# Scale stores, row broadcasts and the first context load in another order on SyncE, with three buffers placed anew

## The chip, the core and the metric

The kernel runs on one core of a Trainium2 chip. The time is that of one execution on the device, in microseconds (us). The core has five engines with queues of their own, which meet only through semaphores: TensorE (PE in the profile; its weight loads are shown as PEld), VectorE (DVE), ScalarE (ACT), GpSimd (POOL) and SyncE (SP). SP does no arithmetic here; it issues nearly every DMA transfer, each at its place in a written order, and a wait in its order holds up all that stands behind. The transfers are then carried out by 16 DMA engines, whose queue is shared by all that SP issues.

## What is computed

x and the context are 16 batches of 64 tokens with 512 features (1024 tokens: 8 tiles of 128). Four residual steps follow one another:

```python
x = x + tanh(g_xattn[0]) * L0_xattn(layernorm(x), ctx, ctx, mask, wq, wk, wv, wo)   # 32 heads, 8 kv heads, rope
x = x + tanh(g_ffn[0])   * L0_ffn(layernorm(x), Wg, Wu, Wd)       # weights to 4 bits, activations to 8
x = x + tanh(g_xattn[1]) * L1_xattn(layernorm(x), ctx, Wq, bq, Wk, bk, Wv, bv)      # attention over channels
x = x + tanh(g_ffn[1])   * L1_ffn(layernorm(x), W_base, b_base, lora_A, lora_B, router_W, ...)
```

In L0_ffn each row of a weight has its own scale: `scale = max(|w|) / 7`, the row is rounded to integers, and the product is multiplied by the scale. There are 1376 rows in Wg, 1376 in Wu and 512 in Wd.

## The kernel before

The program has two blocks, and a barrier of all engines lies between them. The first, attention_block, computes the whole L0 attention, and in its gaps prepares the weights of the FFN and of the second layer. The second, tail_block, does the other three steps, tile by tile, in an order written out by hand for each engine.

**The slots of the first block.** Its main loop runs over 8 kv heads with two head pairs each (NPAIR is 16) and two halves of the tiles: 32 units, U = 0 to 31. In unit U, PE computes the output product of unit U - 1 (output, four tiles, each ended by L492 and counted in s_wo), transposes the probabilities of U (L608), takes the scores of U + 1 (L472), multiplies probabilities and v (L621), and then computes two or three projections for later units (L78 to L80). ScalarE copies the transposed probabilities out of PSUM (L827), the high part of the result (L832), and so on; VectorE adds the output product to x (accumulate, L939) and takes the low parts; GpSimd normalises and rotates.

**SP's order.** SP runs through slots V = 0 to 63, two to a unit. In each it may load the next piece of an FFN weight (load_piece, L326, into xn), store a finished quantised and transposed piece to a scratch tensor in DRAM (store_piece, L335 to L341), and load attention weights (next_weights, L278 to L290). Waits on semaphores in front of these tie it to the pace of the units. A few things have their place by number of slot: at V = 32 (2 * NPAIR), when all pieces of Wg and Wu are through, their scales go to DRAM: w_scale holds them in SBUF by partition, 10 columns of 128 and one of 96 for each weight, and the store writes every scale as an element of 4 bytes (L382, L385). At V = 53 come the small loads of the second layer (load_block1, L1284), and at V = 56 (4 * NPAIR - 8) the 512 scales of Wd (L391), in the same manner. After the loop SP issues the base weight of the last step (L1303, 1 MB; it counts to the same semaphore as the loads of load_block1), the three quantised weights (L398 to L400: w_T twice, wd_T), waits until PE has done the last projection (s_proj), loads tile 0 of the context for the second layer (load_context, L1429: four transfers of 128 KB, two for each parity into b_ctx), waits for the scale stores (s_p_row), and reads the scales back as rows that are broadcast to all partitions (L406: w_row twice, wd_row). At last it duplicates the first q and k (duplicate_tile, L1439) when VectorE has them.

**Who waits for these.** In unit 30, VectorE starts the selection of the experts (selection_of_experts, L1027) and PE the transposes of the small weights; both wait for all loads of load_block1 and the base weight. At the end of unit 30, ScalarE rounds both parities of the context to their high parts (first_split_hi, L801); GpSimd takes the low parts behind them (L1241), and then the inverse deviations (L1245) for which it needs VectorE. PE uses the result in the last output product (first_qk). The rows and quantised weights are used in the second block only.

**The end of the first block.** VectorE's last steps are first_lo_qk for both parities (L1063), the last three accumulates, and between the last two of them low_b_lo (L1069), which waits for ScalarE's low_b_hi (L797). low_b is read in the tail by lora. The first instruction of VectorE in the second block is front_tile of tile 1 (f_xn, L1403).

**Buffers.** late_buffers places the second layer's buffers over those of the attention that are dead by then: before, b_ctx (the raw context) in the large area behind b_qk_hi, and b_xn and b_v over wo_lo, the low parts of the output weights.

Of the kernel before, what the change touches and what calls it, by code (L numbers as in the profile page):

```python
# [20 lines left out]
P = 128  # L21
B, S, D = 16, 64, 512
# [67 lines left out]
def attention_block(cx, K, x_dram, ctx_dram, mask_dram, wq_dram, wk_dram, wv_dram, wo_dram, trig_dram,  # L90
# [4 lines left out]
    with ExitStack() as st:  # L95
# [104 lines left out]
        def n_quant(p):  # L200
            return sum(i[0] != "max" for i in PIECES[:p])

        def n_out(q, b):
            whole = [i for i in PIECES if i[0] != "max"][:q]
            return sum(16 * (2 if i[4] % P else 1) for k, i in enumerate(whole) if k % 2 == b)
# [63 lines left out]
        def _(sp):  # L269
# [99 lines left out]
            for V in range(4 * NPAIR):  # L369
# [7 lines left out]
                next_weights(V // 4, V % 4)  # L377
                if V == 2 * NPAIR:
                    for b in range(2):
                        sp.wait_ge(s_p_out[b], n_out(2 * FT, b))  # L380
                    for w in range(2):
# [5 lines left out]
                                     ).then_inc(s_p_row, 16)  # L387
                if V == 4 * NPAIR - 8:
                    for b in range(2):
                        sp.wait_ge(s_p_out[b], n_out(n_quant(len(PIECES)), b))  # L390
                    sp.dma_start(K.scale_dram[2].rearrange("(r p) -> p r", p=P), w_scale[:, 2 * FT:NSCALE],  # L391
                                 allow_slow_non_contiguous=True).then_inc(s_p_row, 16)
# [8 lines left out]
            sp.wait_ge(s_proj, len(ALL))  # L401
            for par in range(2):
                load_context(sp, M, ctx_dram, 0, par)
            sp.wait_ge(s_p_row, 5 * 16)
            for dst, src in zip(K.W.row + [K.W.row_d], K.scale_dram):
                sp.dma_start(dst[:, :], src.partition_broadcast(P)).then_inc(K.s_w_in, 16)  # L406
            sp.wait_ge(M.s_k_zero, 4)
            for par in range(2):
# [460 lines left out]
        def _(dve):  # L869
# [265 lines left out]
            first_lo_qk(1)  # L1135
            accumulate(last + 2, UT + 2)
            low_b_lo()
            accumulate(last + 3, UT + 3)

# [166 lines left out]
def late_buffers(cx, K):  # L1306
# [6 lines left out]
    M.qk_hi = [free.take(f"b_qk_hi{i}", [P, D], F32R) for i in range(2)]  # L1313
    M.ctx_raw = [free.take(f"b_ctx{i}", [P, D]) for i in range(2)]
    raw = Area(cx.nc, K.area_base, K.raw1_end)
# [54 lines left out]
    late.used = at["wo_lo"]  # L1370
    M.xn, M.v, M.x3 = take("b_xn", [P, D]), take("b_v", [P, DC, P]), two("b_x3", [P, D])
    late.used = at["q_rope0"]
# [1796 lines left out]
```

## Time and profile before

| | us |
|---|---|
| median of 3 runs | 830.22 (829.99 to 832.27) |
| the profiled execution | 829.99 |
| its span in the profile | 828.2 |
| PE busy in the span | 798.5 (96%) |
| VectorE, ScalarE, GpSimd busy | 552.4, 455.6, 500.9 |
| first block | to about 599 |
| second block | from about 599 |

The profile shows one execution. A timeline row gives the start of a group of instructions, its length, engine and line; idle time in front of it stands in brackets with what ended it. The length of a transfer on SP's timeline is the time for its issue; when its data have landed is told by the rows of the transfers. A stretch of the span can be asked for busy time of each engine, granted clock of PE, and for what the DMA engines moved. "Share" is the mean busy share of the 16 DMA engines; it can be over 1 or high with few bytes moved when single packets take long.

### The profile page before, as it was taken

The numbers are of one execution on the slowest core, as the hardware profiler recorded it, in microseconds if no ns is written. First come the engines' busy times: TensorE is split into PE (matmuls) and PEld (weight loads), VectorE is DVE, ScalarE is ACT, GpSimd is POOL, SyncE is SP. The second block draws the span as 40 slices with busy tenths as digits, with TensorE's granted clock in tenths as the row PEclk, the third lists the DMA queues.
The fourth block names the chain that finished last, engine by engine and source line by source line (L and its number), as shares of the span: only waits on it lengthen the run. The fifth ranks groups of instructions, "written<-read, shape, count | busy, mean of one in ns | idle before, by whom it ended". The sixth has DMA issues, their size and how long they took to land. (4 is left out here: it accounts for less than half of the span.)

```text
span 828.2 us, 13922 instructions
## 1 busy us (share of the span) xinstructions
PE 798.5 (96%) x5105; PEld 646.1 (78%) x5105; DVE 552.4 (67%) x1041; ACT 455.6 (55%) x858; POOL 500.9 (60%) x432
## 2 busy tenths in 40 slices
PE   6999999999999999999999999999989999999996
PEld 5878888888888888888888888887646567777874
DVE  4856766556666545566555555557799999998752
ACT  4545455544445444344543443424488898878861
POOL 1587666645656664555775445654277867777752
PEclk9999999999999999999999999999999999999998
DMA  9410332322413232732112200385224331431100
GB/s 294 129 65 26 115 89 51 120 56 77 127 38 90 59 92 79 39 106 62 61 48 78 57 11 26 43 186 202 65 71 103 89 89 47 115 78 46 47 26 25
DMA packets 72259, 66.77 MB, mean 81 GB/s; under 512 B 35920, under 2 KB 51504, under 8 KB 71808
## 3 DMA queue, kind: packets, MB, share of 16 engines
q1 hardware_dynamic: 71520, 65.56, 30.4%
q8 instruction: 41, 0.67, 0.3%
q10 hardware_dynamic: 672, 0.33, 0.1%
q14 instruction: 26, 0.21, 0.1%
HBM read 49.04 MB, written 6.34 MB: 67 GB/s over the span
## 5 line engine op out<-in xcount | busy, mean ns | idle before, releaser
L939 DVE SCALAR_TENSOR_TENSOR x_res<-bank,gate,x_res 128x512 f32<-128x512 f32 x128 | 95.7, 748 | 78.3 <-PE bank L492 77.6
L1182 POOL TENSOR_TENSOR prob<-prob,row_inv 128x512 f32<-128x512 f32 x32 | 33.4, 1044 | 173.6 <-DVE row_inv L935 173.5
L1168 POOL TENSOR_TENSOR rope_swap<-rope_swap,trig 128x512 f32<-128x512 f32 x80 | 103.4, 1293 | 36.8 <-ACT rope_swap L694 36.7
L910 DVE TENSOR_TENSOR rope_cos<-bank,trig 128x512 f32<-128x512 f32 x80 | 54.7, 684 | 86.8 <-PE bank L80 86.8
L78 PE MATMUL bank<-xnT_hi,wq_hi 128*128 128x512 f32 x256 | 103.8, 406 | 0.2 <-DVE xnT_lo L874 0.2
L487 PE MATMUL bank<-wo_hi,oT_hi 128*128 128x512 f32 x256 | 102.0, 398 | 0.6 <-issue 0.5
L693 ACT COPY rope_swap<-bank 64x512 f32<-64x512 f32 x80 | 46.7, 583 | 100.2 <-DVE rope_cos L910 99.7
L80 PE MATMUL bank<-xnT_hi,wq_lo 128*128 128x512 f32 x256 | 101.4, 396 | 0.0
L79 PE MATMUL bank<-xnT_lo,wq_hi 128*128 128x512 f32 x256 | 101.3, 396 | 0.0
L488 PE MATMUL bank<-wo_lo,oT_hi 128*128 128x512 f32 x256 | 100.8, 394 | 0.0
L1174 POOL TENSOR_TENSOR q_rope<-rope_cos,rope_swap 128x512 f32<-128x512 f32 x64 | 83.8, 1309 | 5.0
L2838 POOL TENSOR_TENSOR b_e<-b_e,b_inv 128x512 f32<-128x512 f32 x64 | 68.4, 1079 | 24.9 <-DVE b_inv L2085 24.2
L492 PE MATMUL bank<-wo_hi,oT_lo 128*128 128x512 f32 x256 | 80.6, 396 | 0.2
L827 ACT COPY probT<-bank 128x512 f32<-128x512 f32 x32 | 18.7, 585 | 101.2 <-PE bank L608 101.2
L832 ACT CAST oT_hi<-bank 128x512 fp32r<-128x512 f32 x64 | 34.4, 590 | 70.1 <-PE bank L621 70.1
L472 PE MATMUL bank<-k_rope,q_rope 128*128 128x64 f32 x512 | 61.0, 272 | 0.0
L472 PEld LDWEIGHTS bank<-k_rope,q_rope 128*128 128x128 f32 x512 | 59.8, 192 | 0.5
L487 PEld LDWEIGHTS bank<-wo_hi,oT_hi 128*128 128x128 f32 x256 | 48.2, 188 | 13.9 <-issue 0.9
L492 PEld LDWEIGHTS bank<-wo_hi,oT_lo 128*128 128x128 f32 x256 | 48.0, 188 | 12.2 <-DVE oT_lo L1104 1.1
L78 PEld LDWEIGHTS bank<-xnT_hi,wq_hi 128*128 128x128 f32 x256 | 48.1, 188 | 12.0 <-DVE xnT_lo L874 0.7
L80 PEld LDWEIGHTS bank<-xnT_hi,wq_lo 128*128 128x128 f32 x256 | 48.1, 188 | 11.4
L488 PEld LDWEIGHTS bank<-wo_lo,oT_hi 128*128 128x128 f32 x256 | 48.2, 188 | 10.3 <-issue 0.2
(240 smaller groups left out, 1999.7 us busy)
## 6 DMA issues: line engine op xcount, KB each, us to landing
wq_raw<-in_L_xattn_wq SPq DMA_DIRECT2D x16, 512.0 KB, 4.1
wo_raw<-in_L_xattn_wo SPq DMA_DIRECT2D x16, 512.0 KB, 3.9
xn<-in_L_ffn_Wd SPq DMA_DIRECT2D x16, 256.0 KB, 3.2
b_ctx<-in_ctx SPq DMA_DIRECT2D x32, 128.0 KB, 2.6
b_k_twice<-b_qk_hi SPq DMA_DIRECT2D x32, 128.0 KB, 2.4
w_T_dram<-w_out SPq DMA_DIRECT2D x28, 128.0 KB, 2.4
w_T<-w_T_dram SPq DMA_DIRECT2D x2, 1376.0 KB, 17.8
xn<-in_L_ffn_Wg SPq DMA_DIRECT2D x10, 256.0 KB, 3.9
```

The lines of the kernel that those rows point to most:

```text
L78: pe.matmul(out, a_hi, b_hi, start=first, stop=False)
L79: pe.matmul(out, a_hi, b_lo, start=False, stop=False)
L80: return pe.matmul(out, a_lo, b_hi, start=False, stop=last)
L472: mm = pe.matmul(score[:, n * S:(n + 1) * S], q_rope[jp][:, b], k_rope[:, b * S:(b + 1) * S], start=True, stop=True)
L487: pe.matmul(out, oT_hi[:, tl, h], wo_hi[jp][:, h, :], start=(h == 0), stop=False)
L488: pe.matmul(out, oT_hi[:, tl, h], wo_lo[jp][:, h, :], start=False, stop=False)
L492: mm = pe.matmul(out, oT_lo[:, tl, h], wo_hi[jp][:, h, :], start=False, stop=(h == 1))
L910: dve.tensor_tensor(out=rope_cos[:, rp, :].rearrange("p (b s) -> p b s", s=S), in0=proj[stream % 2][:, :].rearrange("p (b s) -> p b s", s= ...
L939: dve.scalar_tensor_tensor(out=K.x[:, t, :], in0=wo_ps[t % 2][:, :], scalar=K.gate[:, 0:1], in1=K.x[:, t, :], op0=ALU.mult, op1=ALU.add).t ...
L1168: pool.tensor_tensor(out=sw, in0=sw, in1=sin_b, op=ALU.mult).then_inc(s_rope, 1)
L1174: pool.tensor_tensor(out=dst, in0=rope_cos[:, rp, :].rearrange("p (b s) -> p b s", s=S), in1=sw, op=ALU.add).then_inc(s_rope, 1)
L2838: pool.tensor_tensor(out=e[m % 4][:, :], in0=e[m % 4][:, :], in1=inv_total[:, n:n + 1].to_broadcast([P, D]), op=ALU.mult).then_inc(s_w, 1)
```

## The change

It moves instructions on two engines and gives three buffers another place.

- The four stores of the Wg and Wu scales leave slot 32 for slot 56, in front of the store of the Wd scales; one wait for all weight pieces stands before all five.
- After the last projection, SP first waits for the scale stores and issues the three row broadcasts; then it waits until PE has done the output product of unit 29 (s_wo of UT * (2 * NPAIR - 2) = 120), and only then loads tile 0 of the context.
- VectorE does low_b_lo after the last accumulate, not before it.
- b_ctx lies over wo_lo, of which unit 29 is the last reader, and b_xn and b_v where b_ctx was.

```diff
--- before.py
+++ after.py
@@ -375,9 +375,9 @@
                 if (p := piece_at(V - 3)) is not None:
                     store_piece(p)
                 next_weights(V // 4, V % 4)
-                if V == 2 * NPAIR:
+                if V == 4 * NPAIR - 8:
                     for b in range(2):
-                        sp.wait_ge(s_p_out[b], n_out(2 * FT, b))
+                        sp.wait_ge(s_p_out[b], n_out(n_quant(len(PIECES)), b))
                     for w in range(2):
                         sp.dma_start(K.scale_dram[w][0:(FT - 1) * P].rearrange("(r p) -> p r", p=P),
                                      w_scale[:, w * FT:w * FT + FT - 1], allow_slow_non_contiguous=True
@@ -385,9 +385,6 @@
                         sp.dma_start(K.scale_dram[w][(FT - 1) * P:F].unsqueeze(1),
                                      w_scale[0:FL, w * FT + FT - 1:w * FT + FT], allow_slow_non_contiguous=True
                                      ).then_inc(s_p_row, 16)
-                if V == 4 * NPAIR - 8:
-                    for b in range(2):
-                        sp.wait_ge(s_p_out[b], n_out(n_quant(len(PIECES)), b))
                     sp.dma_start(K.scale_dram[2].rearrange("(r p) -> p r", p=P), w_scale[:, 2 * FT:NSCALE],
                                  allow_slow_non_contiguous=True).then_inc(s_p_row, 16)
 
@@ -399,11 +396,12 @@
             sp.dma_start(K.W.T_d[:, 0:FT - 1, :], K.T_dram[2][:, 0:FT - 1, :]).then_inc(K.s_w_in, 16)
             sp.dma_start(K.W.T_d[0:FL, FT - 1, :], K.T_dram[2][0:FL, FT - 1, :]).then_inc(K.s_w_in, 16)
             sp.wait_ge(s_proj, len(ALL))
-            for par in range(2):
-                load_context(sp, M, ctx_dram, 0, par)
             sp.wait_ge(s_p_row, 5 * 16)
             for dst, src in zip(K.W.row + [K.W.row_d], K.scale_dram):
                 sp.dma_start(dst[:, :], src.partition_broadcast(P)).then_inc(K.s_w_in, 16)
+            sp.wait_ge(s_wo, UT * (2 * NPAIR - 2))
+            for par in range(2):
+                load_context(sp, M, ctx_dram, 0, par)
             sp.wait_ge(M.s_k_zero, 4)
             for par in range(2):
                 sp.wait_ge(M.s_qk_lo[par], 1)
@@ -1133,9 +1131,9 @@
             first_lo_qk(0)
             accumulate(last + 1, UT + 1)
             first_lo_qk(1)
-            accumulate(last + 2, UT + 2)
+            for tl in range(2, UT):
+                accumulate(last + tl, UT + tl)
             low_b_lo()
-            accumulate(last + 3, UT + 3)
 
 
         @block.gpsimd
@@ -1311,7 +1309,7 @@
     free.used = K.free_off
     M.h, M.hq, M.hqT = free.take("f_h", [P, F]), free.take("f_hq", [P, F], BF16), free.take("f_hqT", [P, FT, P], BF16)
     M.qk_hi = [free.take(f"b_qk_hi{i}", [P, D], F32R) for i in range(2)]
-    M.ctx_raw = [free.take(f"b_ctx{i}", [P, D]) for i in range(2)]
+    M.xn, M.v = free.take("b_xn", [P, D]), free.take("b_v", [P, DC, P])
     raw = Area(cx.nc, K.area_base, K.raw1_end)
     raw.used = K.raw1_off
     M.x3T_hi, M.x3T_lo = raw.take("b_x3T_hi", [P, DC, P], F32R), raw.take("b_x3T_lo", [P, DC, P], F32R)
@@ -1368,7 +1366,7 @@
     late.used = at["wo_hi"]
     M.gate, M.up = two("f_gate", [P, D]), two("f_up", [P, D])
     late.used = at["wo_lo"]
-    M.xn, M.v, M.x3 = take("b_xn", [P, D]), take("b_v", [P, DC, P]), two("b_x3", [P, D])
+    M.ctx_raw, M.x3 = two("b_ctx", [P, D]), two("b_x3", [P, D])
     late.used = at["q_rope0"]
     M.f_xn, M.xq, M.xqT = take("f_xn", [P, D]), take("f_xq", [P, D], BF16), take("f_xqT", [P, DC, P], BF16)
     M.ctx_split = two("b_ctx_split", [P, D], F32R)
```

SP's order, from slot 56 to the duplicates, before (w_scale is the tile of scales, w_scale_dram their copies in DRAM, b_ctx the raw context):

```order
L391 DMA w_scale_dram<-w_scale 128x4x1
L1303 DMA l_raw_base<-in_L_ffn_W_base 128x4x512
L398 DMA w_T_49<-w_T_dram 128x5504
L398 DMA w_T_50<-w_T_dram 128x5504
L399 DMA wd_T<-w_T_dram 128x5120
L400 DMA wd_T<-w_T_dram 96x512
L1429 DMA b_ctx_72<-in_ctx 64x512 x2
L1429 DMA b_ctx_73<-in_ctx 64x512 x2
L406 DMA w_row_64<-w_scale_dram 128x1376
L406 DMA w_row_65<-w_scale_dram 128x1376
L406 DMA wd_row<-w_scale_dram 128x512
```

And with the change, the same place, up to the base weight (w_T and wd_T follow it as before):

```order
L382 DMA w_scale_dram<-w_scale 128x10x1
L385 DMA w_scale_dram<-w_scale 96x1
L382 DMA w_scale_dram<-w_scale 128x10x1
L385 DMA w_scale_dram<-w_scale 96x1
L388 DMA w_scale_dram<-w_scale 128x4x1
L1301 DMA l_raw_base<-in_L_ffn_W_base 128x4x512
```

And with the change, SP behind wd_T:

```order
L401 DMA w_row_64<-w_scale_dram 128x1376
L401 DMA w_row_65<-w_scale_dram 128x1376
L401 DMA wd_row<-w_scale_dram 128x512
L1427 DMA b_ctx_143<-in_ctx 64x512 x2
L1427 DMA b_ctx_144<-in_ctx 64x512 x2
```

The four stores that stood some 50 instructions earlier are in front of the fifth now, and the base weight, w_T and wd_T come behind all five; w_row and wd_row went ahead of b_ctx.

VectorE's order at the end of the first block, before (x_res is x, which the accumulates add to; b_qk_lo are the low parts of the first q and k):

```order
L1063 SCALAR_TENSOR_TENSOR b_qk_lo_108<-bank,l_bias,b_qk_hi_70 128x512
L939 SCALAR_TENSOR_TENSOR x_res<-bank,gate,x_res 128x512
L1063 SCALAR_TENSOR_TENSOR b_qk_lo_109<-bank,l_bias,b_qk_hi_71 128x512
L939 SCALAR_TENSOR_TENSOR x_res<-bank,gate,x_res 128x512
L1069 SCALAR_TENSOR_TENSOR l_low_b<-bank,l_low_b 64x512
L939 SCALAR_TENSOR_TENSOR x_res<-bank,gate,x_res 128x512
L95 UNCONDITIONAL_BRANCH
```

And with the change:

```order
L1061 SCALAR_TENSOR_TENSOR b_qk_lo_108<-bank,l_bias,b_qk_hi_70 128x512
L937 SCALAR_TENSOR_TENSOR x_res<-bank,gate,x_res 128x512
L1061 SCALAR_TENSOR_TENSOR b_qk_lo_109<-bank,l_bias,b_qk_hi_71 128x512
L937 SCALAR_TENSOR_TENSOR x_res<-bank,gate,x_res 128x512 x2
L1067 SCALAR_TENSOR_TENSOR l_low_b<-bank,l_low_b 64x512
L95 UNCONDITIONAL_BRANCH
```

l_low_b stands behind both accumulates now, as the last instruction of the block.

## Rows read from the trace of the kernel before

**Rows 1.** The page: busy times, and granted clock by fortieths of the span.
```profile
PE 798.5 (96%) x5105; PEld 646.1 (78%) x5105; DVE 552.4 (67%) x1041; ACT 455.6 (55%) x858; POOL 500.9 (60%) x432
...
PEclk9999999999999999999999999999999999999998
```

**Rows 2.** Stretches: start:end, length, busy us of each engine, clock, share, GB/s.
```profile
332.00:349.00 17.00, 17.00 (x107) 14.72 (x106) 8.64 (x14) 7.47 (x13) 7.21 (x7) 1.00 0.74 27
542.00:552.00 10.00, 10.00 (x65) 8.42 (x63) 6.10 (x10) 4.20 (x8) 2.69 (x4) 1.00 0.83 63
552.00:564.00 12.00, 12.00 (x74) 10.02 (x73) 7.73 (x12) 3.34 (x7) 5.42 (x5) 1.00 0.98 399
564.00:576.00 12.00, 11.65 (x76) 9.65 (x74) 7.19 (x19) 4.57 (x8) 7.33 (x10) 1.00 0.61 192
815.00:820.00 5.00, 2.46 (x11) 1.94 (x12) 1.42 (x6) 1.32 (x5) 2.48 (x2) 0.79 0.04 16
```

**Rows 3.** Timeline of SP: start, length, line, transfer; around slot 32.
```profile
329.55 0.41 SPq L382 DMA_DIRECT2D w_scale_dram<-w_scale  x1
...
331.69 0.71 SPq L385 DMA_DIRECT2D w_scale_dram<-w_scale  x1
```

**Rows 4.** Transfers issued 332.4 to 333.1: KB each, us to landing.
```profile
xn<-in_L_ffn_Wd SPq DMA_DIRECT2D x1, 256.0 KB, 17.3
xn<-in_L_ffn_Wd SPq DMA_DIRECT2D x1, 176.0 KB, 17.9
```

**Rows 5.** Timeline of SP, 540 to 569 us.
```profile
540.06 1.28 SPq L391 DMA_DIRECT2D w_scale_dram<-w_scale  x1
541.44 0.45 SPq L1303 DMA_DIRECT2D l_raw_base<-in_L_ffn_W_base  x1
...
543.33 4.03 SPq L399 DMA_DIRECT2D wd_T<-w_T_dram  x1
...
565.93 2.39 SPq L1429 DMA_DIRECT2D b_ctx<-in_ctx  x4
```

**Rows 6.** Transfers by tile; the last line: those issued 565.9 to 568.3.
```profile
w_row<-w_scale_dram SPq DMA_DIRECT2D x2, 688.0 KB, 4.7
wd_T<-w_T_dram SPq DMA_DIRECT2D x1, 1280.0 KB, 21.0
l_raw_base<-in_L_ffn_W_base SPq DMA_DIRECT2D x1, 1024.0 KB, 13.8
...
b_ctx<-in_ctx SPq DMA_DIRECT2D x4, 128.0 KB, 2.6
```

**Rows 7.** Timeline of VectorE, ScalarE, GpSimd; in brackets the idle time before.
```profile
571.52 0.75 DVE L939 SCALAR_TENSOR_TENSOR x_res<-bank,gate,x_res 128x512 f32<-128x512 f32 x1 [0.65 <-PE bank L492]
572.18 0.16 DVE L1027 CAST l_act_f<-l_act_i 128x4 f32<-128x4 int32 x1
...
578.11 1.14 ACT L801 CAST b_ctx_split<-b_ctx 128x512 fp32r<-128x512 f32 x2
...
579.39 2.54 POOL L1241 TENSOR_TENSOR b_ctx_split<-b_ctx,b_ctx_split 64x512 fp32r<-64x512 f32 x2
...
583.20 0.59 ACT L827 COPY probT<-bank 128x512 f32<-128x512 f32 x1 [3.94 <-PE bank L608]
...
585.09 1.02 POOL L1245 TENSOR_TENSOR f_rstd<-f_var_eps,minus_half 128x4 f32<-128x4 f32 x1 [3.17 <-DVE f_var_eps L1081]
```

**Rows 8.** Timeline of VectorE at the end of the first block.
```profile
596.82 0.69 DVE L1069 SCALAR_TENSOR_TENSOR l_low_b<-bank,l_low_b 64x512 fp32r<-64x512 f32 x1 [2.67 <-ACT l_low_b L797]
597.58 0.75 DVE L939 SCALAR_TENSOR_TENSOR x_res<-bank,gate,x_res 128x512 f32<-128x512 f32 x1
599.05 0.55 DVE L1403 TENSOR_SCALAR f_xn<-x_res,meanvar_ffn,f_rstd 128x512 f32<-128x512 f32 x1 [0.72 <-PEq L95]
```

**Rows 9.** The barrier's drains: min/median/max ns, start us.
```profile
L95 DVEq DRAIN  x1: 791/791/791, 597.6 to 597.6; - x1
...
L95 SPq DRAIN  x1: 374/374/374, 598.4 to 598.4; - x1
```

## The prediction, made before the change was timed

> **What bounds the kernel now.** I read the page's busy times and granted clock first, then stretches, then the queue of SyncE (SP), which issues nearly every transfer, then the engines where the changed steps sit. PE is busy for 96% of the span, with a granted clock of 0.9 or more (2.4 GHz is 1.0) in all slices but the last [rows 1], and in the stretches of the first block it is busy for all of it: 17.00 of 17 us, 10.00 of 10, 12.00 of 12 [rows 2]. So in this block the end is set by TensorE, and an edit counts only if PE comes to wait. The first hole is at 564 to 576 (11.65 of 12 us). From about 576 to 599 us the block ends through a chain of short steps, and there a late transfer or copy can reach PE.
>
> **The change, part by part.**
>
> *1. Four scale stores leave slot 32.* They write 4-byte elements: 2 x (10 x 128 + 96) = 2752. SP issued them from 329.55 to 332.40 [rows 3]. Behind them the DMA engines stayed busy and moved almost nothing: 27 GB/s over 332 to 349 us at a share of 0.74 [rows 2]; two weight loads issued at that time landed after 17.3 and 17.9 us [rows 4]. So these elements hold the queue up for some 17 us. But PE was busy for 17.00 of those 17 us: the preparation of the FFN weights has room. What goes away here was on nobody's path: gain 0.
>
> *2. The same stores come to slot 56, ahead of the big loads.* There one store of 512 elements stood already (540.06 us), and it too held things up: 63 GB/s over 542 to 552, then the queue moved 399 GB/s over 552 to 564 [rows 2]. The base weight landed at 541.44 + 13.8 = 555.2, and wd_T, the last of the big ones, at 543.33 + 21.0 = 564.3 [rows 5, 6]. Now 2752 + 512 = 3264 elements stand ahead. SP pays 2.85 us more of issue [rows 3], between 541 and 545, when it next has to wait till 565.93 anyway: 0. How long the elements hold the queue is the unknown. Two points: 512 elements, 10 us (542 to 552); 2752 elements, 17 us (332 to 349). The lower bound is that the small store drains beside the big ones: 17 us, end at 542 + 17 = 559. The upper bound is that they add: 27 us, end at 569. A straight line through the points (7 us for 2240 elements, 0.0031 us each) gives 18.6 us, end at 561. I take 561: the line uses both rows, and the sum of both counts the fixed part of about 8 us twice.
>
> The Trainium skill bears on this ("DMA: Bandwidth & Descriptors", Specifications): below 512 B a DMA engine does a read-modify-write. Read as a cost in proportion to the elements, 17 us / 2752 x 3264 = 20.2 us, the end would be at 562; but the 512 elements would then have held the queue for 3.2 us, and the trace shows 10. So the row speaks against pure proportion; either way the result below is the same side of the limit, with 1.5 us less to spare.
>
> After the elements, in order of issue: the base weight lands 3 us later (555.2 - 552), at 564; everything up to wd_T needs 12.3 us (564.3 - 552), so 573.3. Who waits: VectorE's first instruction of the expert selection starts at 572.18 and needs all block-1 loads, the base weight among them [rows 7]; 564 leaves it 8 us. The first use of w_T lies behind the block's end at 599.05 [rows 8].
>
> *3. The row broadcasts go ahead of tile 0's context, and the context waits for output unit 29.* That wait ends when VectorE can accumulate the unit's last tile, 571.52 [rows 7]; before, the context was issued at 565.93 [rows 5]. Issue now runs from 571.5 to 573.9 (2.39 us). Behind this wait only the duplicates are queued on SP; they need first_qk, which PE does in the last output product, some 15 us later, so the wait costs SP nothing. The wait for the scale stores comes ahead of the rows: they end with the hold-up, 561, before the last projection is done. In the queue, the rows (2 x 688 KB + 256 KB = 1.67 MB) need 4.2 us at 399 GB/s: 577.5. The first half pair of context (0.26 MB) needs 0.7 us more, the second another 0.7; with 1 us for the landing (an undisturbed one lands 2.6 us after issue [rows 6]) they are there at 579.2 and 579.8. Who waits: ScalarE, which starts the two casts at 578.11 [rows 7]. It would wait 1.1 us and end them at about 580.4. Behind the casts on ScalarE is the copy of the transposed probabilities for the last unit, which starts at 583.20 because PE's transposes are that late [rows 7]. So 2.8 us are to spare, and the cost is 0. GpSimd's low parts (2.54 us) then run 580.1 to 582.9 instead of from 579.39; its next piece waited till 585.09 for VectorE [rows 7]. Again 0. This is the point where cover can go: each us by which the elements end after 563.8 is a us on PE.
>
> *4. low_b_lo goes behind the last accumulate.* Before, VectorE waited 2.67 us in low_b_lo for ScalarE, ran it 596.82 to 597.51, and started the last accumulate at 597.58 [rows 8]; PE's last product (L492) is what that one waits for. The accumulate gets earlier by at most the 0.07 us between the two, and by nothing if it was PE that ended last, as in front of the accumulate at 571.52 [rows 7]. low_b_lo now comes after it: VectorE is done 0.69 us later, at 598.39 + 0.69 = 599.08. The block ends in a barrier: VectorE's drain ended at 597.6 + 0.79 = 598.4, SP's at 598.4 + 0.37 = 598.8, and f_xn started at 599.05 [rows 8, 9]. SP was last by 0.4. So 0.4 of 0.69 us are hidden behind SP's last duplicate, and 0.3 are paid. Bounds: 0 (the drain takes the copy in) and 0.69.
>
> *5. Buffers change places* (context to the wo_lo area, xn and v to the area of the context). The tail has the same instructions and waits, so 0; no row suggests that an address matters.
>
> Sum against the profiled execution (829.99 us, span 828.2): 0 + 0 + 0 + 0.3 + 0 = 830.3. It is the lowest of the three times, 0.2 below the median, so the median goes to 830.5.
>
> **The rivals.**
>
> *Slower: the hold-ups add, and the context is late.* If the 512 elements queue up behind the 2752 for their full 10 us, the end is 569, all of part 3 is 8 us later: context at 587.2 and 587.8, casts done at 588.4, and the probability copy starts there and not at 583.20. PE waits 5.2 us in front of its product with v, and all behind it is late by that: 829.99 + 0.3 + 5.2 = 835.5, on the median's scale 835.7. It decides from an end of 563.8 on, and is worth over 0.3% from 566.3. For it speaks that the 512 elements alone cost 10 us, more for each than the 2752; against it that 17 us for 2752 shows the big ones draining side by side. A hole of 5 us could also take PE's clock down to its lower level (1.2 GHz) for a while, as over 815 to 820 us, where PE was busy for 2.46 of 5 us and the granted clock was 0.79 [rows 2]; I put 1 us at the top of the range for it. The base weight would land at 572, just at its limit.
>
> *VectorE alone sets the barrier*, with nothing hidden: 0.69 us, 830.9 in the median. Within 0.3%.
>
> *Faster: the hold-up at 332 us mattered after all.* If the late loads of w_down pieces cost PE time later in their pipeline, taking them away would return something, at most the few us by which PE's work there could be thinner than its rows show (matmul ends are modelled): 827. Against it: PE shows no idle time there at all.
>
> *The change does nothing that shows:* this is the likeliest case, and it ends at 830.5.
>
> **How the numbers follow.** A difference of 0.3% (2.5 us) is about what a measurement of this kernel can tell from no change. No wait reaches PE, or less than 2.5 us do (forecast, the barrier case, and ends up to 566.3): 0.68. The context is late by more: 0.26. Something comes back: 0.06. The likeliest case's own range is 829.3 to 832; the range goes up to the slow rival with its clock: 829.2 to 836.6. The chances are 0.06 faster, 0.68 same, 0.26 slower.
>
> **What would show it.** In the changed kernel's trace: the stretch from 542 us with low GB/s ends near 561 (569 for the rival); b_ctx lands at 579 and ScalarE's casts start there with a wait for a DMA of about 1 us (9 us for the rival); the last probability copy starts at 583.2 (588.4); PE has no hole of over 1 us between 583 and 590 (5 us for the rival); around 332 us the two w_down loads land well before 17 us are over, with PE busy all the time as before; f_xn starts 0.2 us later after the barrier. A wrong prediction would most likely come from the length of the hold-up, which I have from two points of other sizes.

## The result, and the profile after

In the same comparison the changed kernel took 838.40 us (836.81 to 840.86, five runs), the kernel before 831.66 us (829.99 to 832.27, five runs): a ratio of 1.0086, with a 95% interval of 1.0060 to 1.0111 (the ratio takes in all twelve executions of the changed kernel, 834.06 to 840.86). It is slower by 0.86%, about 7.1 us. The forecast (830.5, range 829.2 to 836.6) was wrong. What came true is the rival "the hold-ups add, and the context is late", and it cost more than was put on it.

The profiled execution of the changed kernel took 839.49 us (span 837.7), against 829.99 us (span 828.2) before. The line numbers of the changed kernel are two or three lower than those of the kernel before: the accumulate L939 is L937 here, ScalarE's casts L801 are L799, its probability copy L827 is L825, PE's product with v is L619.

The page of the changed kernel (busy us and shares; granted clock by fortieths), to be read against [rows 1]:

```profile
PE 801.6 (96%) x5105; PEld 649.1 (77%) x5105; DVE 553.8 (66%) x1041; ACT 456.1 (54%) x858; POOL 501.4 (60%) x432
...
PEclk9999999999999999999999999999899999999998
```

PE has as many instructions as before and is busy 3.1 us longer: some of them ran slower. One slice in the 29th fortieth shows the clock. The stretches there in the changed kernel (start:end, length, busy us of PE, weight loads, VectorE, ScalarE, GpSimd, clock, DMA share, GB/s), against [rows 2]:

```profile
329.00:360.00 31.00, 31.00 (x189) 26.44 (x189) 18.94 (x31) 12.56 (x22) 16.50 (x14) 1.00 0.21 69
545.00:552.00 7.00, 7.00 (x46) 5.85 (x46) 4.72 (x8) 2.84 (x5) 1.05 (x1) 1.00 0.78 5
552.00:560.00 8.00, 8.00 (x44) 6.63 (x42) 3.69 (x5) 2.40 (x5) 6.38 (x5) 1.00 0.84 24
560.00:568.00 8.00, 8.00 (x50) 6.63 (x49) 5.10 (x9) 3.49 (x6) 2.13 (x2) 1.00 0.92 73
568.00:576.00 8.00, 8.00 (x51) 6.74 (x51) 5.20 (x17) 1.75 (x3) 5.78 (x9) 1.00 0.92 365
583.00:592.00 9.00, 3.29 (x23) 2.73 (x23) 3.65 (x11) 2.21 (x4) 1.62 (x2) 0.93 0.48 112
592.00:596.00 4.00, 4.00 (x25) 3.63 (x23) 1.93 (x4) 2.46 (x5) 3.77 (x6) 0.50 0.00 0
596.00:600.00 4.00, 4.00 (x17) 3.16 (x15) 2.59 (x6) 1.36 (x3) 0.00 (x0) 0.81 0.00 0
```

Around slot 32 PE is as busy as before, all of the time. From 545 to 568 us the DMA queue moves 5, 24 and 73 GB/s, and only from 568 on 365; before, it was at 399 from 552 on. From 583 to 592 PE works 3.29 of 9 us, and after that hole its clock is down at the lower of its levels (0.50 is 1.2 GHz) for a few us.

SP's own timeline in the changed kernel (start, length of the issue, line, transfer), against [rows 5]:

```profile
541.75 1.01 SPq L382 DMA_DIRECT2D w_scale_dram<-w_scale  x1
...
544.21 1.32 SPq L385 DMA_DIRECT2D w_scale_dram<-w_scale  x1
545.57 0.43 SPq L388 DMA_DIRECT2D w_scale_dram<-w_scale  x1
546.10 0.45 SPq L1301 DMA_DIRECT2D l_raw_base<-in_L_ffn_W_base  x1
...
557.34 0.74 SPq L397 DMA_DIRECT2D wd_T<-w_T_dram  x1
567.71 1.10 SPq L401 DMA_DIRECT2D w_row<-w_scale_dram  x2
568.86 0.71 SPq L401 DMA_DIRECT2D wd_row<-w_scale_dram  x1
573.19 2.39 SPq L1427 DMA_DIRECT2D b_ctx<-in_ctx  x4
```

The landings of these transfers (KB each, us from issue to landing), each read from a stretch around its own issue; against [rows 4, 6]:

```profile
w_scale_dram<-w_scale SPq DMA_DIRECT2D x1, 5.0 KB, 12.6
w_scale_dram<-w_scale SPq DMA_DIRECT2D x1, 0.4 KB, 19.1
w_scale_dram<-w_scale SPq DMA_DIRECT2D x1, 2.0 KB, 22.1
l_raw_base<-in_L_ffn_W_base SPq DMA_DIRECT2D x1, 1024.0 KB, 24.6
wd_T<-w_T_dram SPq DMA_DIRECT2D x1, 96.0 KB, 24.3
w_row<-w_scale_dram SPq DMA_DIRECT2D x2, 688.0 KB, 16.0
wd_row<-w_scale_dram SPq DMA_DIRECT2D x1, 256.0 KB, 20.2
b_ctx<-in_ctx SPq DMA_DIRECT2D x4, 128.0 KB, 14.5
```

The first store lands at 541.75 + 12.6 = 554.4, the fourth (0.4 KB, issued at 544.21) at 563.3, the fifth at 545.57 + 22.1 = 567.7. They finish one behind another: 554.4, 556.3, 560.5, 563.3 and 567.7, with 1280, 96, 1280, 96 and 512 elements. SP's wait ahead of the rows ends at that moment (567.71). The base weight lands at 570.7, the last piece of wd_T at 557.34 + 24.3 = 581.6, the last row at 568.86 + 20.2 = 589.1. The four pieces of the context, issued from 573.19 on, land with the rows and just after them.

The longest of the waits of the changed kernel between 540 and 612 us that has a DMA behind it, and what follows from it (us in total, times, longest):

```profile
ACT b_ctx_split L799 <- DMA b_ctx<-in_ctx: 9.7, 1, 9.7
...
PE bank L619 <- ACT probT L825: 5.7, 1, 5.7
```

And the same chain in the timelines of ScalarE, PE and VectorE (idle time before, and releaser, in brackets), against [rows 7, 8]:

```profile
589.62 1.27 ACT L799 CAST b_ctx_split<-b_ctx 128x512 fp32r<-128x512 f32 x2 [9.73 <-DMA b_ctx<-in_ctx]
590.79 0.58 ACT L825 COPY probT<-bank 128x512 f32<-128x512 f32 x1
...
591.42 2.08 PE L619 MATMUL bank<-probT,v_nat 64*128 64x128 f32 x16 [5.71 <-ACT probT L825]
...
595.62 0.63 PE L486 MATMUL bank<-wo_lo,oT_hi 128*128 128x512 f32 x1
...
607.05 0.75 DVE L937 SCALAR_TENSOR_TENSOR x_res<-bank,gate,x_res 128x512 f32<-128x512 f32 x1 [3.44 <-PE bank L490]
607.83 0.69 DVE L1067 SCALAR_TENSOR_TENSOR l_low_b<-bank,l_low_b 64x512 fp32r<-64x512 f32 x1
608.84 0.55 DVE L1401 TENSOR_SCALAR f_xn<-x_res,meanvar_ffn,f_rstd 128x512 f32<-128x512 f32 x1 [0.32 <-PEq L95]
```

ScalarE stands in the casts of the context, 9.73 us, with the probability copy queued behind them; PE waits 5.71 us for the copy. The product at 595.62 takes 0.63 us where the same kind takes 0.39 at full clock. f_xn, the first instruction behind the barrier, starts at 608.84 and not at 599.05.

**Where 9.8 us come from.** 1.7 us are not the change's. They arise at the head of the program, long before any changed instruction: PE's first projection products take 0.63 us each up to 13.4 us in this execution, and 0.39 from 10.3 us on in the one of the kernel before. The granted clock reads 1.00 there in both profiles, but 0.63 us is what such a product takes further down where it reads 0.50. Which head an execution gets is not tied to the change: e6_pe_filled, below, has the short one with the changed order, and e2_stores_only the long one with the old order. One product from the changed kernel and one from the kernel before:

```profile
12.57 0.63 PE L78 MATMUL bank<-ctxT_hi,wk_hi 128*128 128x512 f32 x1
```
```profile
10.33 0.39 PE L79 MATMUL bank<-ctxT_lo,wk_hi 128*128 128x512 f32 x1
```

The rest is the hole, 5.7, the lower clock behind it, 2.0, and the barrier, 0.3 (the last two are told apart below); together 9.7. The second block is as long as before (228.9 us from f_xn to the end of the span; 229.15 before). Both contain a lower clock near the end of the program; e5_half_back, e6_pe_filled and e8_spread, where PE keeps its clock there, need 226.6 to 226.7 us. Single executions thus differ by 2 to 3 us in parts that the change does not touch.

### The profile page after: what moved, and what is told of

It is laid out like the page before. It is cut to its first block and busy times, and to the rows that moved or that the text cites. A ratio compares the mean times of both kernels' runs of the same rounds, so it can differ in the third digit from the quotient of the medians.

```text
span 837.7 us, 13922 instructions
## 1 busy us (share of the span) xinstructions
PE 801.6 (96%) x5105; PEld 649.1 (77%) x5105; DVE 553.8 (66%) x1041; ACT 456.1 (54%) x858; POOL 501.4 (60%) x432
## 5 line engine op out<-in xcount | busy, mean ns | idle before, releaser
L937 DVE SCALAR_TENSOR_TENSOR x_res<-bank,gate,x_res 128x512 f32<-128x512 f32 x128 | 95.6, 747 | 81.9 <-PE bank L490 81.2
L825 ACT COPY probT<-bank 128x512 f32<-128x512 f32 x32 | 18.8, 586 | 97.5 <-PE bank L606 97.5
L486 PEld LDWEIGHTS bank<-wo_lo,oT_hi 128*128 128x128 f32 x256 | 48.5, 189 | 10.4 <-issue 0.2
```

What stands on the lines that cost most here:

```text
L486: pe.matmul(out, oT_hi[:, tl, h], wo_lo[jp][:, h, :], start=False, stop=False)
L937: dve.scalar_tensor_tensor(out=K.x[:, t, :], in0=wo_ps[t % 2][:, :], scalar=K.gate[:, 0:1], in1=K.x[:, t, :], op0=ALU.mult, op1=ALU.add).t ...
```

## The experiments

Each is timed beside runs of the kernel before on the same chip. First the overview; "casts" is the start of ScalarE's casts of the context, "hole" the idle time of PE ahead of its product with v, "last store" the us from issue to landing of the 2 KB store. In the profiled executions, the casts start 1.5 to 2.2 us later than in the kernel before by the head alone, but for e1_stores_back, e4_low_b_last and e6_pe_filled, which have the short head.

| kernel | us | against before | last store | casts | hole |
|---|---|---|---|---|---|
| before | 831.66 | | | 578.11 | 0 |
| changed | 838.40 | 1.0086 | 22.1 | 589.62 | 5.71 |
| e1_stores_back | 830.62 | 0.9981 | | 577.59 | 0 |
| e2_stores_only | 835.73 | 1.0049 | 20.6 | 584.96 | 0.97 |
| e3_context_first | 834.54 | 1.0034 | 21.8 | 585.86 | 2.56 |
| e5_half_back | 829.47, one execution | | 16.4 | 583.40 | 0 |
| e6_pe_filled | 835.72 | 1.0051 | 21.8 | 588.47 | filled |
| e7_short_rows | 832.17, one execution | | 13.3 | 580.05 | 0 |
| e8_spread | 829.63, one execution | | 4.5 | 579.87 | 0 |
| e9_stores_alone | 837.55, one execution | | 19.5 | 588.04 | 4.34 |

### The stores or the order: each half alone

*The changed kernel with the four stores back at slot 32*:

```diff
-                if V == 4 * NPAIR - 8:
+                if V == 2 * NPAIR:
                     for b in range(2):
-                        sp.wait_ge(s_p_out[b], n_out(n_quant(len(PIECES)), b))
+                        sp.wait_ge(s_p_out[b], n_out(2 * FT, b))
...
+                if V == 4 * NPAIR - 8:
+                    for b in range(2):
+                        sp.wait_ge(s_p_out[b], n_out(n_quant(len(PIECES)), b))
                     sp.dma_start(K.scale_dram[2].rearrange("(r p) -> p r", p=P), w_scale[:, 2 * FT:NSCALE],
```

> The changed kernel with the four Wg and Wu scale stores at slot 32 again; rows, context, low_b_lo and buffers as changed. Theory (hold-up): in the changed kernel 3264 single elements held the transfers up until about 568, the context landed at 589 and ScalarE waited 9.7 us for it, which left PE idle for 5.7 us and then at half clock. Without the four stores the hold-up ends near 552 again, the context lands by 577 and nobody waits: time within 1 us of before, last wait of PE at L619 gone, base weight landing about 14 us after issue. Rival (order): the context is late because it waits for output unit 29 and stands behind 1.67 MB of rows; then ScalarE still waits for it, at least 4 of the 9.7 us, and the time stays 3 us or more above before.

830.62 us (828.12 to 832.90) against 831.69: 0.9981 (0.9957 to 1.0005). The rows, the context's wait for output unit 29 and the moved low_b_lo are all in this kernel, and it is not slower. Its ScalarE and PE have no wait:

```profile
577.59 1.14 ACT L802 CAST b_ctx_split<-b_ctx 128x512 fp32r<-128x512 f32 x2
...
583.42 1.16 PE L622 MATMUL bank<-probT,v_nat 64*128 64x128 f32 x16
```

*The kernel before with only the stores moved*:

```diff
-                if V == 2 * NPAIR:
+                if V == 4 * NPAIR - 8:
                     for b in range(2):
-                        sp.wait_ge(s_p_out[b], n_out(2 * FT, b))
+                        sp.wait_ge(s_p_out[b], n_out(n_quant(len(PIECES)), b))
```

> The kernel before with only the four stores moved to slot 56; the context is still ahead of the rows and is issued after the last projection. Hold-up theory: elements end near 568, the big loads near 581, the context right behind them at 582 to 583 (not 587 to 589), casts done near 584.5, so PE waits 1 to 2 us and keeps its full clock: 1 to 2.5 us above before. If the store move alone carries the whole loss, it is 7 to 9 us above before; if it costs nothing without the new order, it is equal.

835.73 us (831.79 to 837.07): 1.0049 (1.0017 to 1.0081). The hold-up is there with the old order too, and the context waits behind it:

```profile
584.96 0.62 ACT L798 CAST b_ctx_split<-b_ctx 128x512 fp32r<-128x512 f32 x1 [4.61 <-DMA b_ctx<-in_ctx]
...
587.11 1.16 PE L618 MATMUL bank<-probT,v_nat 64*128 64x128 f32 x16 [0.97 <-ACT probT L824]
```

The profiled execution took 832.13 us, with a hole of only 0.97 us and the clock at 1.00 behind it (span 830.3, 2.1 over before: 2.1 more at the head, 1.0 for the hole, 1.1 less in the second block). The median is 3.6 us above it. The mean granted clock on record is 0.998 in the executions of 831.79 and 832.13 us and 0.993 in the three of 835.73 to 837.07. So those three lost clock; where, and whether behind a longer hole, no trace shows.

*The changed kernel with the context issued ahead of the rows* (both waits kept):

```diff
-            sp.wait_ge(s_p_row, 5 * 16)
-            for dst, src in zip(K.W.row + [K.W.row_d], K.scale_dram):
-                sp.dma_start(dst[:, :], src.partition_broadcast(P)).then_inc(K.s_w_in, 16)
             sp.wait_ge(s_wo, UT * (2 * NPAIR - 2))
             for par in range(2):
                 load_context(sp, M, ctx_dram, 0, par)
+            sp.wait_ge(s_p_row, 5 * 16)
+            for dst, src in zip(K.W.row + [K.W.row_d], K.scale_dram):
+                sp.dma_start(dst[:, :], src.partition_broadcast(P)).then_inc(K.s_w_in, 16)
```

> The changed kernel with the context load ahead of the three row broadcasts (still after the wait for output unit 29). Hold-up theory: everything up to wd_T still lands near 582, then the context without the rows' 4 to 5 us in front: ScalarE waits about 5 us rather than 9.7, PE 1 to 2 us rather than 5.7, and the clock does not fall; 1 to 2.5 us above before. Rival (the rows cost nothing, the wait for unit 29 does): no change against the changed kernel, 7 us above before.

834.54 us (830.25 to 837.27): 1.0034 (1.0011 to 1.0057). The hole is 2.56 us (1 to 2 were expected), and the clock stays at 1.00 behind it up to the barrier. It falls only behind the barrier, where PE waits for about 2 us in every kernel here: 0.57 over 604 to 608 us. The same happens over 600 to 604 us in two kernels without a hole (0.65 in e10_spread16, 0.73 in e11_spread32), and not in the kernel before, so that fall is not the hole's. By the medians the new order costs something only on top of the hold-up: nothing alone (0.9981), some 4 us (838.40 against 834.54) with the stores in front. The loss is more than the sum of its halves, 0.49 - 0.19 = 0.30%, against 0.86%. The intervals are too wide to show that alone (0.17 to 0.81, -0.43 to 0.05, and 0.60 to 1.11%), but the holes of the traces say the same: 0.97 us and none, against 5.71.

### What the hole costs beyond itself

*The changed kernel with 20 unused products in front of the wait for the probability copy.* They change nothing that is computed; they keep PE at work in the hole:

```diff
+                if U == 2 * NPAIR - 1:
+                    for i in range(20):
+                        pe.matmul(av[0][:, :], oT_hi[:, i % UT, 0], wo_hi[1][:, 0, :], start=True, stop=True)
                 pe.wait_ge(s_probT_sb, U + 1)
```

> The changed kernel with 20 products of 128x512 that nobody reads, on PE in front of its wait for the last probability copy (4.7 us at full clock; the bank is overwritten by the real product behind them). Theory: PE's idle 5.7 us cost twice, 5.7 us of waiting and then 2.3 us because the granted clock fell to half from 590.6 to 597.4. With PE at work in the hole the granted clock stays at 1.00 from 576 to 600, the products behind run at 0.23 us each, and the time is 2 to 2.5 us below the changed kernel (5 us above before). Rival (the clock falls for another reason, or the slow stretch is a wait in disguise): the clock falls all the same and the time stays.

835.72 us (834.11 to 837.54): 1.0051 (1.0031 to 1.0071), against 1.0086 without them. First the stretch 576 to 600 of the changed kernel, then the same of this one (PE's busy us is the first pair, the clock the third number from the end):

```profile
576.00:600.00 24.00, 17.60 (x97) 13.99 (x93) 14.95 (x31) 9.13 (x19) 6.44 (x8) 0.86 0.47 158
```
```profile
576.00:600.00 24.00, 22.62 (x123) 17.38 (x120) 17.59 (x36) 10.48 (x21) 6.44 (x8) 1.00 0.43 135
...
588.47 1.27 ACT L802 CAST b_ctx_split<-b_ctx 128x512 fp32r<-128x512 f32 x2 [9.06 <-DMA b_ctx<-in_ctx]
...
589.64 0.58 ACT L828 COPY probT<-bank 128x512 f32<-128x512 f32 x1
```

The context is late as before, but the clock does not fall. From the start of the probability copy to f_xn it is 605.69 - 589.64 = 16.05 us here, 608.84 - 590.79 = 18.05 in the changed kernel, and 599.05 - 583.20 = 15.85 in the kernel before. So 2.0 us of the loss are the clock, and 0.2 the barrier and the rest. The other executions agree: their mean granted clock is 0.994 to 0.998 here (five) and 0.988 to 0.995 in the changed kernel (twelve). The Trainium skill ("TensorE: Matmul & The Clock Gate", HAM oscillation) tells of waits for a DMA that take TensorE back to its lower clock. The two stretches above agree: 0.86 with the hole, 1.00 with it filled.

### The moved copy alone

*The kernel before with low_b_lo behind the last accumulate*:

```diff
             accumulate(last + 2, UT + 2)
-            low_b_lo()
             accumulate(last + 3, UT + 3)
+            low_b_lo()
```

> The kernel before with only low_b_lo behind the last accumulate. Prediction's step: VectorE's drain ends 0.69 us later and passes SP's by 0.3 us, so the first instruction after the barrier starts 0.3 us later relative to the last product of PE (before: 599.05 against 596.92 for the last L492, 2.13 us apart; now 2.4). If the drain takes it in: 2.13. If nothing is hidden: 2.8. The time itself can't tell these apart.

827.58 us in one execution. VectorE at the end of its first block, against [rows 8]:

```profile
597.34 0.75 DVE L939 SCALAR_TENSOR_TENSOR x_res<-bank,gate,x_res 128x512 f32<-128x512 f32 x1 [3.44 <-PE bank L492]
598.12 0.69 DVE L1069 SCALAR_TENSOR_TENSOR l_low_b<-bank,l_low_b 64x512 fp32r<-64x512 f32 x1
599.13 0.55 DVE L1403 TENSOR_SCALAR f_xn<-x_res,meanvar_ffn,f_rstd 128x512 f32<-128x512 f32 x1 [0.32 <-PEq L95]
```

The total can't show 0.3 us; the trace can. From PE's last product (596.67) to f_xn it is 2.46 us, 2.13 before: +0.33.

### What in the stores holds the queue

*One of the two weights' stores back at slot 32*, so that 1376 + 512 = 1888 elements stand at slot 56:

```diff
+                if V == 2 * NPAIR:
+                    for b in range(2):
+                        sp.wait_ge(s_p_out[b], n_out(2 * FT, b))
+                    for w in range(0, 1):
...
                 if V == 4 * NPAIR - 8:
...
-                    for w in range(2):
+                    for w in range(1, 2):
```

> The changed kernel with Wg's scale stores (1376 elements) at slot 32 and Wu's at slot 56 with Wd's: 1376 + 512 = 1888 elements ahead of the big loads. What it tells: how the hold-up grows. Known: 512 elements 10 us (before), 3264 elements 23 us (changed kernel). If each element has its price with some 8 us on top (the prediction's line, 8.4 + 0.0031 n), 14 us. If it goes by the same line through the two measured in this place (7.3 + 0.0048 n), 16 to 17 us, base weight landing 18 to 19 us after issue, context at about 582, at most 1 us of wait on PE. If the stores simply add (half of 17 and 10), 18 to 19 us, and PE waits 1 to 3 us.

829.47 us in one execution (before 829.9). The last store:

```profile
w_scale_dram<-w_scale SPq DMA_DIRECT2D x1, 2.0 KB, 16.4
...
583.40 1.27 ACT L809 CAST b_ctx_split<-b_ctx 128x512 fp32r<-128x512 f32 x2 [3.53 <-DMA b_ctx<-in_ctx]
```

Issued at 543.29, it lands at 559.7, 18.0 us behind the first issue (541.70). In the changed kernel 3264 elements take 567.7 - 541.75 = 25.9 us. The 1376 elements between the two cost 7.9 us, 5.7 ns each on the mean. The 18.0 us are at the lower end of the 18 to 19 that were expected if the stores simply add. The 5.7 ns are no price per element, though: by the landings of the changed kernel, its second store of 1280 elements adds 4.2 us, the two of 96 add 2.0 and 2.8, and the last, of 512, adds 4.4. ScalarE waits 3.53 us, and PE not at all (1 to 3 us were expected): with this hold-up the context is late by less than PE's cover.

*The changed kernel, where SP waits for the stores before it issues the base weight*, so that nothing shares the queue with them:

```diff
                 sp.wait_ge(s_wq_lo[par], NQP * HKV)
+            sp.wait_ge(s_p_row, 5 * 16)
             load_base(sp, R1, K.a)
```

> The changed kernel with SP waiting for the five scale stores to land before it issues the base weight and the big loads. If the elements take their 23 us by themselves (one after another), they land near 566 as in the changed kernel, everything behind moves to 580 and later, and the hole on PE is as long or some us longer. If the big loads behind them are what makes them slow (at slot 32, with 432 KB behind, 2752 of them took 17 us), they land by 555 to 560 and the context is earlier: hole under 3 us.

837.55 us in one execution. SP, the last store, and a stretch of it:

```profile
545.28 0.43 SPq L388 DMA_DIRECT2D w_scale_dram<-w_scale  x1
564.85 0.37 SPq L1302 DMA_DIRECT2D l_raw_base<-in_L_ffn_W_base  x1
...
w_scale_dram<-w_scale SPq DMA_DIRECT2D x1, 2.0 KB, 19.5
l_raw_base<-in_L_ffn_W_base SPq DMA_DIRECT2D x1, 1024.0 KB, 7.0
...
552.00:560.00 8.00, 8.00 (x44) 6.66 (x43) 3.69 (x5) 2.23 (x4) 6.30 (x5) 1.00 0.00 0
```

Alone, the stores still need 19.5 us for the last one, against 22.1. So the big loads behind them account for 2.6 us at most; the rest is the stores' own, and the loads are held up by it. And over 552 to 560 us the DMA engines show a share of 0.00 while the stores are under way: the profile records next to no packet in that time. The base weight takes 7.0 us once the stores are done.

*The changed kernel with neighbouring elements 64 bytes apart in DRAM* (and, for the probe, the rows read from other inputs), then *16* and *32 bytes apart*:

```diff
-                        sp.dma_start(K.scale_dram[w][0:(FT - 1) * P].rearrange("(r p) -> p r", p=P),
+                        sp.dma_start(K.wide[w][0:(FT - 1) * P, 0].rearrange("(r p) -> p r", p=P),
...
+    K.wide = [nc.dram_tensor(f"w_scale_dram{i}", (n, 16), F32, kind="Internal").ap() for i, n in enumerate((F, F, D))]
```

> The changed kernel with the same 3264 elements written 64 bytes apart in memory and not next to each other (the rows are read from other inputs of the same size, since the scales are not in one piece; this part is not the reference's). If the hold-up comes from neighbouring elements that share a stretch of memory, the base weight lands in under 18 us after issue and the context is in time. If each element costs by itself wherever it goes, the base weight lands 24 to 25 us after issue as in the changed kernel.

> The same with 16 bytes from one element to the next. If writes meet within 32 bytes, two meet here and the stores land 5 to 10 us after issue; within 64 bytes, four meet and they take longer than at 32 bytes distance, 8 to 15 us; in the changed kernel, with 4 bytes, 13 to 22 us.

> As the kernel with elements 64 bytes apart (there the stores landed 4.5 us after issue, the base weight 7.8 us), but with 32 bytes from one to the next; the rows are read from other inputs, which is not the reference's. If what neighbouring writes share is a stretch of 32 bytes or less, all is as with 64: stores land in 4 to 5 us. If it is 64 bytes, two writes meet in each and a part of the hold-up is back: 6 to 12 us for the stores.

Times 829.63, 829.83 and 832.70 us, one execution each. The last store at 64 bytes and the stretch 552 to 560 of that kernel, then the last store at 16 and at 32 bytes:

```profile
w_scale_dram<-w_scale SPq DMA_DIRECT2D x1, 2.0 KB, 4.5
...
552.00:560.00 8.00, 8.00 (x43) 6.60 (x42) 3.69 (x5) 2.46 (x5) 6.39 (x5) 1.00 1.03 432
```
```profile
w_scale_dram<-w_scale SPq DMA_DIRECT2D x1, 2.0 KB, 6.7
```
```profile
w_scale_dram<-w_scale SPq DMA_DIRECT2D x1, 2.0 KB, 4.5
```

The same 3264 elements of 4 bytes, with the same issue time on SP, land in 4.5 us when 64 or 32 bytes lie between their starts, in 6.7 at 16 bytes, in 22.1 when they touch. It is not their number that holds the queue, and not that there are five stores; it is that neighbours are written singly so close together. Two things go with the distance here and are not told apart: how many elements share the same few bytes, and how much DRAM all of them cover (13 KB when they touch, 209 KB at 64 bytes). In all three the context's casts start without a wait. (832.70 at 32 bytes has no hole either: its second block is 229.5 us long, against 226.7 at 64 bytes, with the clock down behind the barrier and again near the end of the program, 0.54 over 820 to 824 us.)

*The changed kernel with whole short rows*: each partition writes its scales in one piece, 40 bytes for the two weights and 16 for the third, the two stores of 96 elements left as they were. The order of the scales in DRAM is then another.

```diff
-                        sp.dma_start(K.scale_dram[w][0:(FT - 1) * P].rearrange("(r p) -> p r", p=P),
-                                     w_scale[:, w * FT:w * FT + FT - 1], allow_slow_non_contiguous=True
+                        sp.dma_start(K.scale_dram[w][0:(FT - 1) * P].rearrange("(p r) -> p r", p=P),
+                                     w_scale[:, w * FT:w * FT + FT - 1]
...
```

> The changed kernel with the scales stored by partition: 40 and 16 bytes in a row where single 4-byte elements were scattered, so 2 x (128 + 96) + 128 = 576 pieces, not 3264, of nearly the same bytes (the rows then hold scales in a wrong order; this part of the computation is not the reference's). Theory (the number of single elements holds the queue up): the stretch of low GB/s ends some 5 to 10 us after the issue, the context lands before 580, no wait for it on ScalarE. Rival (the five stores cost by their number, or by the place in the order): base weight still lands over 20 us after issue.

832.17 us in one execution. From issue to landing the five stores need 3.1, 3.1, 7.2, 11.1 and 13.3 us, the base weight 17.0 (changed kernel 24.6). Some of the hold-up goes, and the context comes in time. But the hold-up ends 15.6 us behind the first issue (5 to 10 were expected) for 576 pieces, where 3264 need 25.9: it does not go by the number of pieces. What the remaining 13.3 us of the last store are made of (its own 16-byte neighbours, or the 4-byte ones ahead) was not separated.

## Why the prediction was wrong

Its frame held: TensorE sets the end, and an edit costs something only where it makes PE wait. By its steps:

1. *Stores leave slot 32, gain 0.* Right. PE is busy 31.00 of 31 us over 329 to 360, and e1_stores_back, which has them there again, is as fast as the kernel before. The two w_down loads issued there land after 3.2 and 3.1 us now, as forecast, and nothing is gained by it. The rival "faster" falls with it.
2. *The hold-up ends at 561, on a straight line through two points.* **This is the step that failed.** Set back by the 1.7 us of the head, the stores began when before's single one did, 540.06, and landed at 566.0: 25.9 us and not 20.9. Of the 5.0 us too little, 2.1 are the four stores (563.3 - 541.75 = 21.6 us; at slot 32 it was 349 - 329.55 = 19.5), and 2.8 the 512 elements behind them: they add 4.4 us, and the line gave them 1.6. The line mixed a count with a place: its two points come from different slots with other traffic, and its slope, 3.1 ns, is not the 5.7 ns that e5_half_back and the changed kernel give at this one. Nor does the time go by elements alone, as the landings one by one show. The bound above, 569, held; the truth lay 5.0 us above the line and 3.0 below the sum. The remark that each us behind 563.8 is a us on PE was right: 566.0 is 2.2 behind, and with step 3's misses that makes the hole.
3. *Rows and context need 5.9 us behind the big loads, 2.8 us to spare, cost 0.* The order is harmless as such (e1_stores_back). The sizes were low: the big loads took 581.6 - 567.7 = 13.9 us (12.3), rows and context 589.6 - 581.6 = 8.0 us (5.9). Too little by 1.6 and 2.1. Both could have been read from the kernel before. wd_T has a last piece of 96 KB behind the one of 1280 KB, which the 12.3 us left out; it landed at 547.40 + 19.2 = 566.6, and not 564.3:

```profile
wd_T<-w_T_dram SPq DMA_DIRECT2D x1, 96.0 KB, 19.2
```

And the rows, issued from 568.37 on, took until 569.48 + 6.0 = 575.5, or 7.1 us for 1.67 MB (235 GB/s, worked out from these), not 4.2 at 399 GB/s. The context is 10.4 us later than forecast: 1.7 head + 5.0 + 1.6 + 2.1. Without the head 8.7, less the 2.8 to spare: a hole of 5.9, measured 5.71. Alone, the miss of step 2 would have made a hole of 2.2 us and the misses of this step one of 0.9; each used the cover that the other counted on.
4. *low_b_lo, +0.3.* Right: +0.33 alone, and f_xn's wait is 0.32 in the changed kernel too.
5. *Buffers, 0.* Right, as far as e1_stores_back can tell.
6. *The base weight is in time.* Right, by less than thought: 570.7, and VectorE's selection starts at 573.86, straight behind an accumulate.

The slow rival had the hole at 5.2 us (5.71) and the casts done at 588.4 (590.9, less the head 589.2); its clock term was 1 us and measured 2.0. That its hole fits is in part luck: its hold-up ends 3.0 us too late (569, measured 566.0), and its rows and loads are 1.6 + 2.1 us too short. It was given 0.26 because 17 us for 2752 elements was read as "the big loads drain side by side with them". e9_stores_alone shows what that row meant: the DMA share of 0.74 during a hold-up is the held-up loads, and the stores need nearly all of their time (19.5 of 22.1 us) with or without them. Two hold-ups in one queue came closer to their sum than to an overlap.

The Trainium skill ("DMA: Bandwidth & Descriptors", Specifications) says that a DMA engine does a read-modify-write below 512 B. That rule by itself does not give the loss: the elements of e8_spread are as small, and land in 4.5 us. The runs agree with it only so far as writes that share their few bytes are the dear ones.

**What stays open.** The parts of the profiled execution that belong to the change sum to 8.0 us (5.7 + 2.0 + 0.3), the ratio says 7.1 with an interval of 5.0 to 9.2. The mean granted clocks (0.988 to 0.995 in the twelve executions of the changed kernel, 0.992 to 1.000 in 28 of the kernel before) say that most executions lose clock somewhere; that it is behind the hole is shown for one. Why e3_context_first (830.25 to 837.27) and e2_stores_only spread so widely is open. Why touching elements are so slow no view shows. No kernel tried is faster than the one before by more than can be measured.

## What to carry to other kernels

A store of single 4-byte elements that touch in DRAM held the queue for 10 us and more here, some of it with no packet on record; put it where the transfers behind it have slack, as at slot 32, and never together with another one in front of a load with a due time. Better, if the reader can take that, write them at least 32 bytes apart (last store 4.5 us for 22.1) or in longer pieces (13.3). What reading the rows back from elements that lie apart would cost, no run shows: the probes read other inputs. And when two hold-ups meet in a queue, add their times until a run shows that they overlap (here the sum was 3 us too much, the line 5 us too little); price the hole that may follow with TensorE's clock on top.

## What the runs showed of the hardware that was not expected

- Single 4-byte writes into DRAM: the last of five stores (3264 elements) lands 22.1 us after its issue with neighbours 4 bytes apart, 6.7 at 16 bytes, 4.5 at 32 and at 64.
- A store can be under way for 8 us with a DMA share of 0.00 and 0 GB/s (e9_stores_alone, 552 to 560 us); a low rate at a high share, as in the changed kernel, is the loads behind it.
- PE's clock: a hole of 5.71 us was followed by 0.50 and 0.81 in the next two stretches of 4 us, one of 4.34 us (e9_stores_alone) by 0.83 over 592 to 596 us, one of 2.56 us (e3_context_first) by none up to the barrier; behind 5.71 us the fall cost 2.0 us. Twenty products that nobody reads took it back, 0.35% of the kernel.
- The wait of about 2 us at the barrier is followed by a lower clock in some executions (e3_context_first 0.57, e10_spread16 0.65, e11_spread32 0.73) and by none in others with the same wait.
- Two executions can differ by 1.7 us at the head of the program alone, by when PE's products come down from 0.63 to 0.39 us, and by up to 3 us in the second block (226.6 to 229.7), by its clock; sums that compare two profiled executions have to take that out first.
